# Experts of a mixture: every token through all four experts, or tokens sorted by expert into 19 tiles with weights copied for each tile

## The chip, the cores and the metric

One Trainium2 chip; the kernel runs on one of its cores. The metric is the device time of one execution in microseconds (us). The kernel before takes 2626.05 us (median of 3 runs, 2625.26 to 2626.93).

## What is computed

The reference sends 2048 tokens of 128 channels through eight residual layers: softmax attention, a spline feed-forward, retention, the spline again, linear attention, a conv-attention layer with a mixture of experts, an RWKV layer, and the conv-attention layer with the experts a second time (same weights). All is float32. The change concerns the mixture, which runs twice:

```
h = layernorm(x)                        # 2048 x 128
expert_idx = argmax(h @ router_w)       # one of E = 4 experts for each token
for e in range(E):
    gv = h @ expert_wv[e]               # 128 -> 2 * 512: gate and value
    gate_raw, value = split(gv, 2)
    y = gate_raw * sigmoid(gate_raw) * value @ expert_proj[e]   # 512 -> 128
    out = out + where(expert_idx == e, y, 0)
```

Only the output of the token's own expert counts.

## The kernel before

The program is a sequence of blocks; in each, the five engines have their own instruction streams, joined by semaphores, and all engines meet at a block's end. Tokens lie as NT = 16 tiles of 128 rows. `experts_stage` (L2018) is one such block and is called twice from `conv_moe_layer` (L2254), the first time followed by the RWKV layer, the second time by `store_stage`.

Its steps. **Norm**: VectorE and ScalarE normalise `moe_y` into `h`, TensorE transposes `h` (L377) into four banks, ScalarE writes them out as `h_t` (called ln_t in the profile, L346). **Router**: 16 small products `h_t` x `router` (L2049) give `logits_ps`; VectorE picks the expert of each token (L2107 to L2114: the maximum, then three chained operations for each expert) as a 0/1 mask `pick`. **Experts**: a loop over NQ = 4 blocks of 512 tokens, unrolled once and then a hardware loop; in it the 4 experts, and for each NF = 4 slices of 128 of the 512 hidden units. Each slice is one product for gate (L2067) and one for value (L2068), both with `expert_wv` in the array and 512 tokens streamed; ScalarE applies Silu (L2094), VectorE multiplies by value (L2147) into `hidden`. After the four slices the down product (L2057) puts 16 products of 128x128x128 into `expert_ps`; VectorE multiplies them by the token's `pick` and adds them into `X` (L2125, four instructions). So all 2048 tokens go through all 4 experts:

```
2067  nc.tensor.matmul(gp[g % 2][:], w["expert_wv"][:, e, f * P:(f + 1) * P], rhs, start=True, stop=True)
2068  nc.tensor.matmul(vp[g % 2][:], w["expert_wv"][:, e, DFF + f * P:DFF + (f + 1) * P], rhs, start=True, stop=True)
2057  ins = nc.tensor.matmul(op[e % 2][:, s * P:(s + 1) * P], hid[:, e % 2, f, s * P:(s + 1) * P],
                             w["expert_proj"][:, e % E, f, :], start=f == 0, stop=f == NF - 1)
2125  nc.vector.scalar_tensor_tensor(xi, op[e % 2][:, s * P:(s + 1) * P], pick[:, bass.ds(i, 1), e % E], xi, ALU.mult, ALU.add)
```

What sets the order is the text of each engine's stream: the down product of an expert stands after slice 1 of the next one, gate and value have two banks each, `hidden` two buffers. GpSimd adds `moe_y` into `X` once (L2084). SyncE has nothing to do in this block. The statistics for the next norm (L2136, L254) close the block. All weights are in SBUF from the first block on (loaded from GpSimd's queue, L832).

`spline_ffn_stage` (L1208) is another block, called twice; SyncE is idle in it as well.

## Time and profile before

| | |
|---|---|
| median of 3 runs | 2626.05 us |
| the profiled execution's own time | 2619.52 us |
| its span, first to last instruction | 2617.8 us |
| TensorE / VectorE / ScalarE / GpSimd busy | 83% / 69% / 53% / 14% |
| granted TensorE clock, mean | 0.918 |
| first experts block, from its first gate product to the next block | 1641.3 to 1816.1 us |
| second one, to the store of the result | 2438.3 to 2612.3 us |

A line of the page's fifth part, or of a view of lines, gives: source line, engine, operation, output<-inputs, shapes, count | busy time, mean ns | idle time of that engine before it and what ended it. In a timeline a line is: start, duration, engine, source line, operation, count [idle before <-releaser]. "PEld" is the weight load of a matmul, "issue" a wait for nothing that the profile shows, and a name with q (SPq, PEq) is an engine's instruction queue. A float32 product appears as two matmul instructions.

### The profile page before, as it was taken

The page shows a single profiled execution, that of the slowest core. Times are in us where ns is not written, and L with a number is a line of the kernel's source. Part 1 is how long each engine was busy: PE and PEld are TensorE (multiplying, and loading weights), DVE is VectorE, ACT ScalarE, POOL GpSimd, SP SyncE. Part 2 cuts the span into 40 slices and gives each one's busy share as a digit, 9 for nine tenths or more (in the row PEclk, how much of TensorE's full clock was granted, in tenths as well). Part 3 has the DMA queues.
Part 4 walks back from the last instruction along what each step waited for, and adds up shares of the span by engine and source line. Part 5 has one row for each costly group of instructions (what it writes and reads, how often), then busy time and mean ns, then how long its engine had stood idle before and what let it go on. Part 6 is the DMA issues. An engine that isn't in the chain of part 4 may idle for free. (4 is left out here: it accounts for less than half of the span.)

```text
span 2617.8 us, 39805 instructions
## 1 busy us (share of the span) xinstructions
PE 2182.6 (83%) x13356; PEld 951.5 (36%) x13356; DVE 1807.8 (69%) x4562; ACT 1384.6 (53%) x1981; POOL 354.5 (14%) x598
## 2 busy tenths in 40 slices
PE   3589999956799747758999998999448999999998
PEld 2123332224444335522233323665222233323665
DVE  7688788647477765678878874334968878884443
ACT  3246656772599743334566666223543566667222
POOL 4000010010355302100002001000000001001000
PEclk8799999987799868869999999999669999999899
DMA  7601010001111000160011000000151011000000
GB/s 196 140 1 38 2 38 1 1 1 36 40 46 49 23 0 1 28 185 13 2 37 38 1 1 1 1 0 0 28 161 37 1 38 34 6 1 2 1 1 16
DMA packets 46128, 81.67 MB, mean 31 GB/s; under 512 B 6132, under 2 KB 34164, under 8 KB 45284
## 3 DMA queue, kind: packets, MB, share of 16 engines
q1 hardware_dynamic: 40464, 70.46, 10.7%
q0 software_dynamic: 2528, 5.65, 0.8%
q10 hardware_dynamic: 2976, 3.55, 0.5%
q8 instruction: 85, 1.39, 0.2%
q14 instruction: 75, 0.61, 0.1%
HBM read 56.18 MB, written 23.07 MB: 30 GB/s over the span
## 5 line engine op out<-in xcount | busy, mean ns | idle before, releaser
L1026 ACT ACTIVATE probs<-score 128x1024 f32<-128x1024 f32 x960 | 825.7, 897 | 528.6 <-PE score L1090 525.4
L1148 DVE TENSOR_REDUCE max_part<-stat 128x1 f32<-128x512 f32 x1152 | 721.8, 683 | 120.2 <-PE stat L1040 118.8
L1103 PE MATMUL pv<-probs,v_ones 128*9 128x512 f32 (+3 forms) x3840 | 443.6, 534 | 0.7 <-ACT out_turned L1017 0.5
L1145 DVE CUSTOM_DVE_ANT_0 masked_scores<-stat,mask_row 128x128 f32<-128x128 f32 (+3 forms) x768 | 343.1, 487 | 101.5 <-PE stat L1040 100.1
L1040 PE MATMUL stat<-first_group_k,first_group_q 128*128 128x512 bf16 (+2 forms) x960 | 302.7, 370 | 78.7 <-DVE max_part L1148 34.2
L1000 POOL TENSOR_SCALAR_AFFINE_SELECT probs<-probs 128x256 f32<-128x256 f32 x384 | 154.8, 408 | 1254.7 <-ACT probs L1026 1251.3
L1040 PE MATMUL stat<-group_k,group_q 128*128 128x512 bf16 (+2 forms) x960 | 288.5, 349 | 15.0 <-DVE max_part L1148 8.9
L1090 PE MATMUL score<-first_group_q,first_group_k 128*128 128x512 bf16 x960 | 262.0, 356 | 15.7 <-DMA first_group_q<-row_max_turned 14.7
L1090 PE MATMUL score<-group_q,group_k 128*128 128x512 bf16 x960 | 253.9, 350 | 5.1 <-DMA group_q<-row_max_turned 2.8
L2094 ACT ACTIVATE gate<-gate_ps 128x512 f32<-128x512 f32 x128 | 76.4, 597 | 262.5 <-PE gate_ps L2067 262.5
L1040 PEld LDWEIGHTS stat<-first_group_k,first_group_q 128*128 128x128 bf16 x960 | 93.9, 99 | 262.0 <-DVE max_part L1148 123.3
L1740 ACT ACTIVATE abs_act_ps<-abs_act_ps 128x1024 f32<-128x1024 f32 (+3 forms) x176 | 167.5, 952 | 27.2 <-PE abs_act_ps L1693 27.0
L2147 DVE TENSOR_TENSOR hidden<-value_ps,gate 128x512 f32<-128x512 f32 x128 | 88.4, 691 | 109.0 <-PE value_ps L2068 108.5
L1090 PEld LDWEIGHTS score<-first_group_q,first_group_k 128*128 128x128 bf16 x960 | 72.8, 98 | 237.8 <-ACT probs L1026 107.9
L1040 PEld LDWEIGHTS stat<-group_k,group_q 128*128 128x128 bf16 x960 | 92.7, 97 | 164.7 <-DVE max_part L1148 67.6
L1090 PEld LDWEIGHTS score<-group_q,group_k 128*128 128x128 bf16 x960 | 69.3, 97 | 221.5 <-ACT probs L1026 169.4
L1774 DVE TENSOR_REDUCE abs_part<-abs_dve_ps 128x512 f32 (+5 forms) x224 | 108.5, 515 | 45.3 <-PE abs_dve_ps L1707 44.2
L2067 PE MATMUL gate_ps<-ln_t,expert_wv 128*128 (+1 forms) x256 | 134.7, 608 | 0.2
L2068 PE MATMUL value_ps<-ln_t,expert_wv 128*128 (+1 forms) x256 | 132.7, 600 | 0.0
L2057 PEld LDWEIGHTS expert_ps<-expert_proj,hidden 128*128 128x128 f32 x1024 | 119.2, 192 | 17.7 <-issue 17.7
L2057 PE MATMUL expert_ps<-expert_proj,hidden 128*128 128x128 f32 x1024 | 119.6, 275 | 1.8 <-DVE hidden L2147 1.8
L1693 PE MATMUL abs_act_ps<-head_k,head_q 128*128 128x512 bf16 x352 | 101.0, 374 | 7.0 <-ACT abs_act_ps L1740 4.0
(330 smaller groups left out, 2318.7 us busy)
## 6 DMA issues: line engine op xcount, KB each, us to landing
q_parts<-parts_t SPq DMA_DIRECT2D x40, 384.0 KB, 3.9
group_k<-k_parts SPq DMA_DIRECT2D x18, 384.0 KB
group_q<-q_parts SPq DMA_DIRECT2D x18, 384.0 KB
k_parts<-parts_t SPq DMA_DIRECT2D x16, 384.0 KB, 4.6
head_q<-q_parts SPq DMA_DIRECT2D x48, 96.0 KB
head_k<-k_parts SPq DMA_DIRECT2D x48, 96.0 KB
first_group_k<-k_parts SPq DMA_DIRECT2D x9, 384.0 KB
first_group_q<-q_parts SPq DMA_DIRECT2D x9, 384.0 KB
```

Source lines behind the costliest of these rows:

```text
L1000: nc.gpsimd.affine_select(tile, tile, [[0, 2], [1, P]], ALU.is_ge, 0.0, base=0, channel_multiplier=-1).then_inc(cut.sem, 1)
L1026: nc.scalar.activation(probs[:, n % PSLOTS, :, 0:width], sc[hp][:, :, 0:width], ACT.Exp, scale=scale).then_inc(expd.sem, 1)
L1040: last = nc.tensor.matmul(out[:, 0:width], uq[b][:, h, at:at + P], uk[b][:, h, c * BANK:c * BANK + width], start=True, stop=True)
L1090: last = nc.tensor.matmul(sc[hp][:, i, 0:BANK - f], uk[b][:, h, kt * P:(kt + 1) * P], uq[b][:, h, j * BANK + f:(j + 1) * BANK], start=True ...
L1103: last = nc.tensor.matmul(acc[32 * h:32 * h + D + 1, f:BANK], v9[:, kt, g * HG + h, :], probs[:, (2 * t + h // 2) % PSLOTS, h % 2, 0:BANK ...
L1145: nc.vector.tensor_tensor_reduce(masked[:, at % 2, 0:width], ring[n % RBANKS][:, 0:width], w["mask_row"][:, BANK - width:BANK], 1.0, NEG, ...
L1148: nc.vector.reduce_max(into, ring[n % RBANKS][:], AX.X).then_inc(stat_used.sem, 1)
L1740: nc.scalar.activation(ps, ps, ACT.Abs, accum_out=part[:, bass.ds(h, 1), i, 0:1]).then_inc(a_used.sem, 1)
L1774: nc.vector.tensor_reduce(part[:, bass.ds(h, 1), i, slot:slot + 1], d_ps[n % DRING][:, 0:width], AX.X, ALU.add, apply_absolute_value=True) ...
L2057: ins = nc.tensor.matmul(op[e % 2][:, s * P:(s + 1) * P], hid[:, e % 2, f, s * P:(s + 1) * P], w["expert_proj"][:, e % E, f, :], start=f = ...
L2067: nc.tensor.matmul(gp[g % 2][:], w["expert_wv"][:, e, f * P:(f + 1) * P], rhs, start=True, stop=True).then_inc(upped.sem, 1)
L2068: nc.tensor.matmul(vp[g % 2][:], w["expert_wv"][:, e, DFF + f * P:DFF + (f + 1) * P], rhs, start=True, stop=True).then_inc(upped.sem, 1)
```

## The change

Both calls of `experts_stage` are rewritten. After the router, VectorE and two small products (with `keep_kq` and with a matrix of ones) compute for each token a slot in an order sorted by expert, in which each expert begins at a multiple of 128, and for each of SLOTS = 19 tiles the expert that owns it (`owner`). GpSimd scatters the rows of `h`, each with its token's number as a 129th element, into a DRAM buffer of 2432 rows: 16 indirect DMAs of 128 rows. SyncE reads them back sorted (5 DMAs). TensorE transposes them, ScalarE applies the norm's affine. Then 19 tiles: SyncE reads the owner into a register and copies that expert's 512 KB of `expert_wv` from SBUF to one of four SBUF buffers; TensorE reads the owner too, makes 8 products of 128x128x128 for gate and value and 4 for the output; ScalarE and VectorE do one Silu, one product and one copy; GpSimd scatters the tile's 128 output rows to a second DRAM buffer at the token's number, by the numbers read back with the rows. At the end SyncE reads 2048 rows (4 DMAs) and VectorE adds them to `x`. Rows that no token fills carry numbers from 2048 up, so they land behind the part that is read; these numbers come from an input that SyncE copies, in the first spline block, into both DRAM buffers (2 x 1.26 MB, DRAM to DRAM). The add of `moe_y` moves from GpSimd to VectorE. The loop is fully unrolled and 19 tiles are always run, however the tokens fall. The diff, cut:

```diff
+SLOTS = NT + E - 1
...
+            @block.sync
+            def _(sp):
+                for dst, rows in copies:
+                    sp.dma_start(dst.rearrange("(p a) c -> p (a c)", p=P), rows.rearrange("(p a) c -> p (a c)", p=P)).then_inc(copied.sem, 16)
+                if copies:
+                    sp.wait_ge(copied.sem, copied.at(16 * len(copies)))
+
...
+        ones = k.sb("ones", [P, P], F32, ctx)
+        steps = k.sb("tile_numbers", [P, SLOTS], F32, ctx)
+        rows = k.sb("sorted_rows", [P, SLOTS, C + 1], F32, ctx)
+        rows_t = k.sb("sorted_t", [P, SLOTS * P], F32, ctx)
...
-        hid = k.sb("hidden", [P, 2, NF, BANK], F32, ctx)
+        hid = k.sb("hidden", [P, 2, BANK], F32, ctx)
+        outs = k.sb("expert_rows", [P, SLOTS, C], F32, ctx)
+        back = k.sb("token_rows", [P, NT, C], F32, ctx)
+        wv = k.sb("tile_wv", [P, WBUFS, 2 * DFF], F32, ctx)
         lp = k.ps("logits_ps", [P, BANK], ctx)
...
+            @block.sync
+            def _(sp):
+                sp.dma_start(steps[:], w["tile_numbers"].partition_broadcast(P)).then_inc(numbered.sem, 16)
+                with nc.allow_non_contiguous_dma(reason="a number for each row"):
+                    sp.dma_start(h[:, :, C], w["token_numbers"]).then_inc(numbered.sem, 16)
+
+                def load_wv(j):
+
+                    e = sp.value_load(owner[0:1, j:j + 1], min_val=0, max_val=E - 1)
+                    if j >= WBUFS:
+                        sp.wait_ge(upped.sem, upped.at(2 * (j - WBUFS) + 2))
+                    sp.dma_start(wv[:, j % WBUFS, :], w["expert_wv"][:, bass.ds(e, 1), :].rearrange("p o f -> p (o f)")).then_inc(wv_in[j % WBUFS].sem, 16)
+
+                sp.wait_ge(owner_ready.sem, owner_ready.at(1))
+                for j in range(WBUFS):
+                    load_wv(j)
+                sp.wait_ge(sorted_out.sem, sorted_out.at(16 * NT))
+                by_tile = sorted_dram.rearrange("(j p) c -> p j c", p=P)
+                for b in range(NB):
+                    js = slice(block_tiles(b)[0], block_tiles(b)[-1] + 1)
+                    sp.dma_start(rows[:, js, :], by_tile[:, js, :]).then_inc(rows_in[b].sem, 16)
+                for j in range(WBUFS, SLOTS):
+                    load_wv(j)
+                sp.wait_ge(returned.sem, returned.at(16 * SLOTS))
+                for q in range(NQ):
+                    ts = slice(QC * q, QC * q + QC)
+                    sp.dma_start(back[:, ts, :], out_dram[0:T].rearrange("(t p) c -> p t c", p=P)[:, ts, :]).then_inc(rows_in[q].sem, 16)
+
+            @block.gpsimd
+            def _(pool):
+                nc.gpsimd.memset(ones[:], 1.0).then_inc(ranked.sem, 1)
+                pool.wait_ge(numbered.sem, numbered.at(32))
+                pool.wait_ge(slot_ready.sem, slot_ready.at(1))
+                norm.wait_rows(pool)
+                for i in range(NT):
+                    nc.gpsimd.indirect_dma_start(sorted_dram, bass.IndirectOffsetOnAxis(ap=slot[:, i:i + 1], axis=0), h[:, i, :], None).then_inc(sorted_out.sem, 16)
+                for j in range(SLOTS):
+                    pool.wait_ge(rows_in[j // QC].sem, rows_in[j // QC].at(16))
+                    pool.wait_ge(out_ready.sem, out_ready.at(j + 1))
+                    nc.gpsimd.indirect_dma_start(out_dram, bass.IndirectOffsetOnAxis(ap=rows[:, j, C:C + 1].bitcast(I32), axis=0), outs[:, j, :], None).then_inc(returned.sem, 16)
...
+                pe.wait_ge(counted.sem, counted.at(1))
+                pe.wait_ge(ranked.sem, ranked.at(1))
+                nc.tensor.matmul(lp[:, NT * E:NT * E + E], w["keep_kq"][:], count[:], start=True, stop=True)
+                nc.tensor.matmul(lp[:, NT * E + E:NT * E + 2 * E], ones[:], count[:], start=True, stop=True).then_inc(ranked.sem, 1)
+
+                def turn(b):
+                    pe.wait_ge(rows_in[b].sem, rows_in[b].at(16))
+                    if b > 0:
+                        pe.wait_ge(kept.sem, kept.at(b))
+                    for s, j in enumerate(block_tiles(b)):
+                        ins = nc.tensor.transpose(tp[:, s * P:(s + 1) * P], rows[:, j, 0:C], w["ident"][:])
+                    ins.then_inc(turned.sem, 1)
+
+                def up(j):
+                    pe.wait_ge(wv_in[j % WBUFS].sem, wv_in[j % WBUFS].at(16 * (j // WBUFS + 1)))
+                    if j >= 2:
+                        pe.wait_ge(hid_ready.sem, hid_ready.at(j - 1))
+                    for bank, first in ((gp[j % 2], 0), (vp[j % 2], DFF)):
                         for f in range(NF):
-                            ins = nc.tensor.matmul(op[e % 2][:, s * P:(s + 1) * P], hid[:, e % 2, f, s * P:(s + 1) * P],
-                                                   w["expert_proj"][:, e % E, f, :], start=f == 0, stop=f == NF - 1)
+                            ins = nc.tensor.matmul(bank[:, f * P:(f + 1) * P], wv[:, j % WBUFS, first + f * P:first + (f + 1) * P], rows_t[:, j * P:(j + 1) * P], start=True, stop=True)
+                        ins.then_inc(upped.sem, 1)
+
+                def down(j, e):
+                    pe.wait_ge(hid_ready.sem, hid_ready.at(j + 1))
+                    if j >= 2:
+                        pe.wait_ge(out_ready.sem, out_ready.at(j - 1))
+                    for f in range(NF):
+                        wgt = w["expert_proj"][:, bass.ds(e, 1), f, :].rearrange("p o c -> p (o c)")
+                        ins = nc.tensor.matmul(op[j % 2][:, 0:C], hid[:, j % 2, f * P:(f + 1) * P], wgt, start=f == 0, stop=f == NF - 1)
                     ins.then_inc(downed.sem, 1)
 
...
+                turn(0)
+                pe.wait_ge(owner_ready.sem, owner_ready.at(1))
+                before = None
+                for j in range(SLOTS):
+                    e = pe.value_load(owner[0:1, j:j + 1], min_val=0, max_val=E - 1)
+                    if j % QC == 0:
+                        pe.wait_ge(kept.sem, kept.at(j // QC + 1))
+                    up(j)
+                    if j % QC == 1 and j // QC + 1 < NB:
+                        turn(j // QC + 1)
+                    if j > 0:
+                        down(j - 1, before)
+                    before = e
+                down(SLOTS - 1, before)
...
-            @block.gpsimd
-            def _(pool):
-                norm.wait_read(pool)
-                nc.gpsimd.tensor_tensor(x[:], x[:], y[:], ALU.add).then_inc(added.sem, 1)
...
+                def keep(b):
+                    js = block_tiles(b)
+                    act.wait_ge(turned.sem, turned.at(b + 1))
+                    nc.scalar.activation(rows_t[:, js[0] * P:(js[-1] + 1) * P], tp[:, 0:len(js) * P], ACT.Identity,
+                                         bias=norm.affine[1][:, 0:1], scale=norm.affine[0][:, 0:1]).then_inc(kept.sem, 1)
+
+                keep(0)
+                for j in range(SLOTS):
+                    act.wait_ge(upped.sem, upped.at(2 * j + 1))
+                    if j >= 4:
+                        act.wait_ge(hid_ready.sem, hid_ready.at(j - 3))
+                    nc.scalar.activation(gate[:, j % 4, :], gp[j % 2][:], ACT.Silu).then_inc(gated.sem, 1)
+                    if j % QC == 1 and j // QC + 1 < NB:
+                        keep(j // QC + 1)
...
+                nc.vector.tensor_reduce(count[:], pick[:], AX.X, ALU.add).then_inc(counted.sem, 1)
+                dve.wait_ge(numbered.sem, numbered.at(32))
+                dve.wait_ge(ranked.sem, ranked.at(2))
+                upto, total = lp[:, NT * E:NT * E + E], lp[:, NT * E + E:NT * E + 2 * E]
+                chain(nc.vector.tensor_copy(begin[:], total))
+                chain(nc.vector.scalar_tensor_tensor(over[:], bcast(steps[:, 0:NT], 1, E), float(P), bcast(begin[:], 2, NT), ALU.mult, ALU.is_lt))
+                chain(nc.vector.tensor_reduce(tiles[:], over[:], AX.X, ALU.add))
+                chain(nc.vector.tensor_tensor_scan(ends[:], ones[:, 0:E], tiles[:], 0.0, ALU.mult, ALU.add))
+                chain(nc.vector.tensor_tensor(begin[:], ends[:], tiles[:], ALU.subtract))
+                chain(nc.vector.scalar_tensor_tensor(begin[:], begin[:], float(P), upto, ALU.mult, ALU.add))
+                chain(nc.vector.tensor_tensor(begin[:], begin[:], count[:], ALU.subtract))
+                for e in range(E):
+                    ins = nc.vector.tensor_tensor_scan(place[:, e, :], ones[:, 0:NT], pick[:, e, :], begin[:, e:e + 1], ALU.mult, ALU.add)
+                chain(ins)
+                chain(nc.vector.tensor_tensor(place[:], place[:], pick[:], ALU.mult))
+                chain(nc.vector.tensor_reduce(at[:], place[:].rearrange("p e t -> p t e"), AX.X, ALU.add))
+                nc.vector.tensor_scalar(slot[:], at[:], -1.0, None, ALU.add).then_inc(slot_ready.sem, 1)
+                chain(nc.vector.tensor_tensor(passed[:], bcast(steps[0:1, :], 2, E - 1), bcast(ends[0:1, 0:E - 1], 1, SLOTS), ALU.is_ge))
+                chain(nc.vector.tensor_reduce(owner_f[:], passed[:], AX.X, ALU.add))
+                nc.vector.tensor_copy(owner[:], owner_f[:]).then_inc(owner_ready.sem, 1)
+                nc.vector.tensor_tensor(x[:], x[:], y[:], ALU.add).then_inc(added.sem, 1)
+
+                def take(j):
+                    dve.wait_ge(downed.sem, downed.at(j + 1))
+                    nc.vector.tensor_copy(outs[:, j, :], op[j % 2][:, 0:C]).then_inc(out_ready.sem, 1)
+
+                for j in range(SLOTS):
+                    dve.wait_ge(gated.sem, gated.at(j + 1))
+                    dve.wait_ge(upped.sem, upped.at(2 * j + 2))
+                    if j >= 2:
+                        dve.wait_ge(downed.sem, downed.at(j - 1))
+                    nc.vector.tensor_tensor(hid[:, j % 2, :], vp[j % 2][:], gate[:, j % 4, :], ALU.mult).then_inc(hid_ready.sem, 1)
+                    if j > 0:
+                        take(j - 1)
+                take(SLOTS - 1)
...
-                        nc.vector.scalar_tensor_tensor(xi, op[e % 2][:, s * P:(s + 1) * P], pick[:, bass.ds(i, 1), e % E], xi,
-                                                       ALU.mult, ALU.add).then_inc(out_used.sem, 1)
...
+                for q in range(NQ):
+                    ts = slice(QC * q, QC * q + QC)
+                    dve.wait_ge(rows_in[q].sem, rows_in[q].at(32))
+                    nc.vector.tensor_tensor(x[:, ts, :], x[:, ts, :], back[:, ts, :], ALU.add).then_inc(completed.sem, 1)
+                    stats.follow(dve, q, completed)
...
+        sorted_dram = [nc.dram_tensor(f"sorted_rows{n}", (SLOTS * P, C + 1), F32, kind="Internal").ap() for n in range(2)]
+        out_dram = nc.dram_tensor("expert_rows", (T + SLOTS * P, C), F32, kind="Internal").ap()
...
-        spline_layer(k, w, x)
+        spline_layer(k, w, x, [(s, d["c_unused_rows"]) for s in sorted_dram])
...
+        "c_tile_numbers": np.arange(SLOTS, dtype=np.float32),
+        "c_token_numbers": np.ascontiguousarray(np.arange(T, dtype=np.int32).reshape(NT, P).T).view(np.float32),
+        "c_unused_rows": np.concatenate([np.zeros((SLOTS * P, C), np.int32), T + np.arange(SLOTS * P, dtype=np.int32)[:, None]], 1).view(np.float32),
```

## Rows read from the trace of the kernel before

**Rows 1.** Page, first part: busy us of each engine (share of the span) xinstructions.
```profile
PE 2182.6 (83%) x13356; PEld 951.5 (36%) x13356; DVE 1807.8 (69%) x4562; ACT 1384.6 (53%) x1981; POOL 354.5 (14%) x598
```
**Rows 2.** Windows, both experts blocks: stretch, length, engines' busy us, granted clock, DMA share, GB/s.
```profile
1641.30:1816.10 174.80, 171.15 (x770) 106.72 (x769) 70.07 (x175) 39.70 (x66) 0.00 (x0) 0.98 0.00 0
2438.30:2612.30 174.00, 170.21 (x769) 106.23 (x768) 70.11 (x175) 39.71 (x66) 0.00 (x0) 0.99 0.00 0
```
**Rows 3.** Chain that ended last, in order of time, second block: start, us, what.
```profile
2438.34 1.91 PE gate_ps L2067 x2
2440.25 1.71 PE value_ps L2068 x2
...
2461.25 3.57 PE expert_ps L2057 x32
2464.82 0.86 PE gate_ps L2067 x2
...
2471.69 3.57 PE expert_ps L2057 x32
```
**Rows 4.** Waits, longest first, 1615 to 1780 us: who waited for whom, us, times, longest.
```profile
ACT gate L2094 <- PE gate_ps L2067: 108.5, 53, 4.7
DVE hidden L2147 <- PE value_ps L2068: 44.9, 47, 2.0
```
**Rows 5.** Timeline of VectorE in the picking of the experts, second block.
```profile
2438.89 0.19 DVE L2112 TENSOR_TENSOR pick<-logits,best 128x16 f32<-128x16 f32 x1
2439.11 0.19 DVE L2113 TENSOR_TENSOR pick<-pick,not_picked 128x16 f32<-128x16 f32 x1
```
**Rows 6.** Timeline, TensorE: a stretch at half clock, then transposes at full clock.
```profile
552.11 2.07 PE L465 MATMUL project<-wT,turned 128*128 128x128 f32 x8
553.98 1.01 PE L457 MATMUL turn<-ident,qkv 128*128 128x128 f32 x4
...
1622.31 0.60 PE L457 MATMUL turn<-ident,qkv 128*128 128x128 f32 x4
```
**Rows 7.** Windows: granted clock (third from the right) in stretches of one kind.
```profile
552.00:554.00 2.00, 2.00 (x11) 1.89 (x10) 0.00 (x0) 0.65 (x2) 0.00 (x0) 0.50 0.04 8
1655.00:1660.00 5.00, 5.00 (x35) 4.04 (x35) 1.68 (x5) 0.60 (x1) 0.00 (x0) 1.00 0.01 3
1140.00:1145.00 5.00, 0.00 (x0) 0.00 (x0) 0.59 (x1) 0.88 (x3) 0.00 (x0) 0.50 1.05 362
24.00:32.00 8.00, 3.45 (x14) 1.83 (x12) 3.90 (x8) 6.43 (x13) 8.00 (x15) 1.00 0.98 249
```
**Rows 8.** Timeline of GpSimd: DMAs that it issues.
```profile
13.69 0.54 POOL L832 DMA_DIRECT2D raw_weights<-in_L_attn_b_Wk  x1
32.10 1.18 POOL L832 DMA_DIRECT2D expert_proj<-in_L_ffn_expert_proj  x1
```
**Rows 9.** DMA issues: out<-in, queue, count, KB each, us from issue to landing.
```profile
q_parts<-parts_t SPq DMA_DIRECT2D x40, 384.0 KB, 3.9
out<-X SPq DMA_DIRECT2D x1, 1024.0 KB, 5.1
```
**Rows 10.** The instructions of tile X and of tile parts_t: landing times, last line of each.
```profile
DMA to landing us min/median/max: 5.1/5.8/6.5
DMA to landing us min/median/max: 2.6/4.0/6.8
```
**Rows 11.** Timeline: the last norm operations before the spline block and the block after it.
```profile
562.66 0.17 DVE L307 TENSOR_SCALAR ln_std<-row_mv 128x16 f32<-128x16 f32 x1 [0.60 <-DVEq L447]
605.77 0.18 DVE L307 TENSOR_SCALAR ln_std<-row_mv 128x16 f32<-128x16 f32 x1 [0.32 <-PEq L1222]
```
**Rows 12.** Timeline: what closes the second block.
```profile
2609.57 1.13 DVE L2125 SCALAR_TENSOR_TENSOR X<-expert_ps,pick,X 128x128 f32<-128x128 f32 x4 [3.18 <-PE expert_ps L2057]
...
2612.30 0.42 SPq L2179 DMA_DIRECT2D out<-X  x1
```
**Rows 13.** Lines of VectorE: an operation on two SBUF inputs, mean ns behind the comma.
```profile
L760 DVE TENSOR_TENSOR qkv<-qkv,cos 128x1024 f32<-128x1024 f32 x8 | 9.8, 1225 | 0.3
```

152 lines of the change are left out of this document (62 added, 90 removed).

## The prediction

> **What bounds the kernel now.** I read the page first: TensorE is busy for 83% of the span, more than any other engine [rows 1]. Then the windows over the two experts blocks: of 174.8 and 174.0 us TensorE works 171 and 170, at a granted clock of 0.98 and 0.99, while VectorE has 70 us of work, ScalarE 40, GpSimd and the DMA engines none [rows 2]. The list of waits says the same from the other side: ScalarE and VectorE wait for the gate and value products [rows 4]. So inside these blocks the time is TensorE's work, and the chain gives its prices [rows 3]: a gate or value product (128x128 weights, 512 tokens) 0.86 us, the down product of an expert (16 products of 128x128x128, 32 instructions) 3.57 us, so 0.1116 us an instruction. One expert on one block of 512 tokens is 8 x 0.86 + 3.57 = 10.44 us, as the two down products 10.44 us apart show, and a block of the program has 16 of them: 167.1 us. The first products are slow (1.91 and 1.71 us in place of 0.86: about 2 us lost), the rest is the end. Everything outside the two blocks is some 2270 us that the change hardly touches.
>
> **What it removes.** All 16 x 10.44 us, the start and the end: the 174.4 us of a block (mean of rows 2) are replaced whole. What comes instead has four stretches one after another.
>
> **1. Routing to slots.** The picks stay, minus one. A chained VectorE operation on 16 columns comes every 0.22 us [rows 5]: copy, maximum, 11 picks, count are 14 x 0.22 = 3.1. Two small products (4 instructions) with the engine at half clock: the transposes behind eight such instructions began 553.98 - 552.11 = 1.87 us after them, 0.23 each [rows 6], in a stretch at clock 0.50 [rows 7]; 4 x 0.23 and a hop there and back are 1.2. Then 14 more operations: 3.1. Sum 7.4 us. The token numbers (2048 pieces of four bytes) are asked for at the block's start, 13 us before the router is done; I cost them at nothing, covered by the norm. If that cover is too short, every us late is a us here. The owner of the tiles and the add of `moe_y` (2 x 1.225 = 2.5 us [rows 13]) come behind the slots on VectorE, beside GpSimd's work: nothing.
>
> **2. Scatter and read back.** GpSimd issues 16 indirect DMAs in a row. The trace has none. A plain DMA of 128 rows costs GpSimd 0.54 us, the one with the most pieces (`expert_proj`, 16 runs of 512 B for each partition) 1.18 us [rows 8]. An indirect one must also read 128 numbers and make 128 addresses; I take 1.18, the dearer row, 18.9 us in all, with 0.54 as the low end; upwards no row bounds it (see the third rival). The last must land: 3.9 us, as stores of `q_parts` to DRAM [rows 9], between 2.6 and 6.8 [rows 10]. SyncE's wait for it holds its five row loads; 3.9 us for the first. Then four transposes at 0.25, and ScalarE's pass: 1.9 with the hops. Sum 18.9 + 3.9 + 3.9 + 1.9 = 28.6 us. The first four weight copies (2 MB) start in this stretch; at the 249 GB/s of rows 7 they take 8.4 us, hidden.
>
> **3. Nineteen tiles.** Each has 12 products of 128x128x128, 24 instructions: 24 x 0.1116 = 2.68 us, 50.9 in all. Fifteen transposes at 0.15 [rows 6] are 2.2, the slow start 2. Nothing else on TensorE should be on the path: gate and value of tile j+1 (1.79 us) stand between those of j and the down product of j, and Silu and the multiply need about 1.3 us. VectorE has 0.69 + 0.3 us a tile, GpSimd 1.2. Reading the owner into a TensorE register is not in the trace. It is covered by the 0.89 us of the down product that is queued; between nothing and the 2.6 us of the shortest DMA in rows 10 I take 1.2, so 0.3 sticks out: 5.7 us, ends 0 and 32. The weight copies: 512 KB and the 64 KB of a scatter at 249 GB/s are 2.4 us a tile, less than the 3.1 of this sum, and four buffers give each copy three tiles of lead, so SyncE's waits for freed buffers hold up nobody. Sum 50.9 + 2.2 + 2 + 5.7 = 60.8 us.
>
> **4. The end.** The last copy 0.3, the issue 1.2, landing in DRAM 5.1 (the store of the result [rows 9]), four loads of 256 KB that together are the load of X: 6.5 [rows 10], an add of 0.69, statistics 0.87 + 0.38 [rows 12] and hops 0.3: 15.3 us. SyncE's last wait holds these loads, which wait for all 19 scatters.
>
> **The sum** is 7.4 + 28.6 + 60.8 + 15.3 = 112.1 us against 174.4: 62.3 less, twice 124.6. The two copies in the first spline block (2.5 MB, 10 us at 249 GB/s, counting each byte once, 20 twice) have 43 us between the two norms [rows 11], with a SyncE that is idle; nothing, unless they run on few DMA engines. From the profiled execution's 2619.5 us this leads to 2494.9; its time lies 6.5 us under the median, so against the median of 2626.05 I forecast **2501 us**. About 0.2% (5 us) is what a measurement of this kernel can tell from no change.
>
> The rows let VectorE's add of `moe_y` and GpSimd's scatters run side by side, since no row shows them together. The Trainium skill's page "SBUF — State Buffer", section "Who interferes with whom", says that a VectorE instruction with two SBUF inputs contends with a GpSimd instruction that reads SBUF. By it the scatters would stand still for those 2.5 us in each block, and the sum would be 2506.
>
> **The forecast's own range.** Low: scatters at 0.54 (-10.2), register read hidden (-5.7), landings of 2.6 (-3.8): 19.7 a block, 2462. High: a register read of 2 us (+15 a block) or scatters at 1.9 (+12): 2530.
>
> **Rivals.**
> *Weights set the pace.* All DMA rates here are between DRAM and SBUF. The copies go from SBUF to SBUF; if that passes the same side of the memory twice and runs at half of 249 GB/s, a tile needs 4.7 us instead of 3.2. 19 x 1.5 = 29 a block: 2559. For: 512 KB for 2.7 us of work is near the rate of rows 7. Against: another stretch there ran at 362 GB/s.
> *The clock.* TensorE stands still for 30 us in stretch 2, and in the tiles it may wait a little each time. Where it had no work, the granted clock was 0.50, the 1.2 GHz level [rows 7]; the first products of the block now ran at it and then rose [rows 3]. If it doesn't rise, a tile is 24 x 0.23 = 5.5 us in place of 2.68: 19 x 2.8 = 54 a block, 2609. Against: an engine that is its own bound is busy throughout. The Trainium skill tells of this in "TensorE: Matmul & The Clock Gate", section "HAM oscillation", of a kernel that waited for DMA in each round and started each one cold; by it this case comes with the first rival, as it stands.
> *Slower.* GpSimd's cost p of an indirect DMA stands in the path 16 times, and from about 3.2 us on it paces the tiles too: a block is then 7.4 + 9.7 + 2 + 14.1 + 36 p. It equals the 174.4 us of now at p = 3.9 us. At 5 us a block takes 213: 2704. For: software makes 128 addresses each time, and no row shows it. Against: the dearest DMA issue of rows 8 is 1.18 us.
> *No change*, because the change doesn't do what it says: should the DRAM-to-DRAM copies run on one engine of 16 (249 / 16 = 15.6 GB/s, 161 us), the spline block grows by 118 and nearly all is given back: 2619. That the tiles don't save work is excluded, since 19 are run whatever the tokens are.
>
> **How the numbers follow.** Forecast 0.62, weights 0.18, clock 0.10, slower 0.06, copies exposed 0.04. The time is the forecast's. The range goes from the low end just worked out, 2460, past the weights' case to 2595; it leaves out the clock, the slow scatter and the exposed copies, 0.2 together. Faster by over 0.2%: 0.62 + 0.18 + 0.10 and half of the copies' case, 0.92; same 0.02; slower 0.06.
>
> **What would show it.** The scatters' issues on GpSimd 1.2 us apart between the slots and SyncE's row loads; the first tile's product some 36 us after the router; products of one tile every 3 to 3.2 us; clock near 1.0 behind the first two tiles; a spline block as long as now. TensorE waiting for `tile_wv` means the first rival, a clock of 0.50 in the tiles the second, GpSimd's issues over 3 us apart the third. The prediction is wrong if a block takes over 150 us or under 92.

## The result and the profile after

| | before | after |
|---|---|---|
| median (4 runs each, side by side) | 2626.49 us (2625.26 to 2630.1) | **2485.8 us** (2480.75 to 2501.3) |
| ratio, 95% interval | | 0.9472 [0.9428, 0.9516] |
| profiled execution, own time / span | 2619.52 / 2617.8 us | 2488.74 / 2487.0 us |
| first experts block, from one norm's `ln_std` to the next | 187.3 us | 117.9 us |
| an experts block from the router's end [rows 2] | 174.8, 174.0 us | 105.1, 104.7 us |

The kernel is 5.3% faster; 2501 us was forecast, 2460 to 2595 as the range. Here is the page's first part of the kernel after, which answers to [rows 1]:

```profile
PE 1956.2 (79%) x12778; PEld 851.6 (34%) x12778; DVE 1734.1 (70%) x4426; ACT 1338.5 (54%) x1901; POOL 416.4 (17%) x668
```

TensorE lost 226 us of work, but the kernel only 131 (profile against profile): TensorE now waits inside the blocks. The windows, the same view as [rows 2, 7], are the two whole blocks, then the scatters, then the tiles:

```profile
1649.30:1754.40 105.10, 57.42 (x479) 56.55 (x479) 33.39 (x106) 17.90 (x27) 35.43 (x35) 0.76 0.38 139
2376.80:2481.50 104.70, 57.20 (x479) 56.34 (x479) 33.42 (x106) 17.89 (x27) 35.39 (x35) 0.76 0.39 140
1660.00:1680.00 20.00, 0.00 (x0) 0.00 (x0) 0.00 (x0) 0.00 (x0) 14.58 (x16) 0.50 0.39 142
1695.00:1735.00 40.00, 40.00 (x361) 40.00 (x360) 14.30 (x30) 10.59 (x17) 13.42 (x14) 1.00 0.50 196
```

So 57 us of TensorE work in 105 us. While GpSimd scatters, TensorE does nothing and its clock stands at 0.50; in the tiles it is busy the whole 40 us at clock 1.00, with the DMA engines half busy. What releases what at the start of the first block is in the timeline of the kernel after:

```profile
1656.30 0.17 DVE L2233 TENSOR_SCALAR slot<-place 128x16 int32<-128x16 f32 x1
...
1656.94 2.27 DVE L2237 TENSOR_TENSOR X<-X,moe_y 128x2048 f32<-128x2048 f32 x1
1657.36 2.83 POOL L2121 DMA_INDIRECT sorted_rows<-ln,slot  x1 [20.62 <-DVE slot L2233]
...
1660.49 0.98 POOL L2121 DMA_INDIRECT sorted_rows<-ln,slot  x1 [0.30 <-issue]
1661.78 0.96 POOL L2121 DMA_INDIRECT sorted_rows<-ln,slot  x1 [0.30 <-issue]
...
1678.19 0.96 POOL L2121 DMA_INDIRECT sorted_rows<-ln,slot  x1 [0.30 <-issue]
1680.47 2.60 SPq L2106 DMA_DIRECT2D sorted_rows<-sorted_rows  x5
1683.33 1.11 PE L2148 MATMUL sorted_ps<-ident,sorted_rows 128*128 128x128 f32 x4 [29.91 <-DMA sorted_rows<-sorted_rows]
1685.31 2.08 PE L2157 MATMUL gate_ps<-sorted_t,tile_wv 128*128 128x128 f32 x8 [0.87 <-ACT sorted_t L2191]
```

Read it as a relay: the slots are ready at 1656.47; sixteen scatters follow, the first of 2.83 us, the others 1.26 us apart (0.96 of work and 0.30 of "issue"); 2.3 us after the last one was begun its rows are in DRAM and SyncE reads them back; 2.9 us later TensorE turns them, and the first gate product starts 36.0 us after the router's end. The chain that ended last shows the second block's end (start, us, what):

```profile
2465.82 0.91 PE expert_ps L2166 x8
...
2467.80 0.48 POOL expert_rows L2125
...
2469.06 2.25 DMA expert_rows<-expert_rows,sorted_rows
2471.33 0.37 SPq L2112
...
2472.29 4.22 DMA token_rows<-expert_rows
...
2476.53 0.69 DVE X L2256
```

Put beside the prediction's four stretches, second block (the middle boundary is the first gate product, at 2412.80; the last product ended at 2467.9, the store was issued at 2481.49):

| stretch | predicted | measured |
|---|---|---|
| 1. Routing to slots | 7.4 | 7.2 |
| 2. Scatter and read back | 28.6 | 28.8 |
| 3. Nineteen tiles | 60.8 | 55.1 |
| 4. The end | 15.3 | 13.6 |
| sum | 112.1 | 104.7 |

Two blocks save 139 us. The profiled execution saved 131: the other 8 are in blocks that the change doesn't touch (the first softmax block 549.5 us in place of 546.6, the softmax of the conv layer 543.1 in place of 537.4). These blocks differ as much between the kernels measured here, none of which changes them: the first softmax block takes 546.5 to 551.8 us, the softmax of the conv layer 535.1 to 549.1. The last experiment bears on that.

### The profile page after: what moved, and what is told of

It is laid out like the page before. It is cut to its first block and busy times, and to the rows that moved or that the text cites. A ratio compares the mean times of both kernels' runs of the same rounds, so it can differ in the third digit from the quotient of the medians.

```text
span 2487.0 us, 38310 instructions
## 1 busy us (share of the span) xinstructions
PE 1956.2 (79%) x12778; PEld 851.6 (34%) x12778; DVE 1734.1 (70%) x4426; ACT 1338.5 (54%) x1901; POOL 416.4 (17%) x668
## 5 line engine op out<-in xcount | busy, mean ns | idle before, releaser
L2248 DVE TENSOR_TENSOR hidden<-value_ps,gate 128x512 f32<-128x512 f32 x38 | 26.3, 691 | 115.6 <-PE value_ps L2157 115.6
L1109 PEld LDWEIGHTS pv<-probs,v_ones 128*9 128x9 f32 x3840 | 57.3, 88 | 112.6 <-issue 91.7
L1662 POOL TENSOR_SCALAR own_positive<-own_scores 128x2048 f32<-128x2048 f32 x16 | 85.7, 5358 | 0.0
L1722 PE MATMUL abs_dve_ps<-head_k,head_q 128*128 128x512 bf16 (+2 forms) x224 | 66.7, 314 | 0.6
L1151 DVE DVE_READ_ACCUMULATOR2_ANT max_part<- 128x1 f32 x768 | 63.6, 83 | 0.1
L1177 DVE RECIPROCAL inv_denominator<-stat 128x16 f32<-128x16 f32 x48 | 12.4, 257 | 69.4 <-PE stat L1056 68.7
```

Source lines behind the costliest of these rows:

```text
L1109: last = nc.tensor.matmul(acc[32 * h:32 * h + D + 1, f:BANK], v9[:, kt, g * HG + h, :], probs[:, (2 * t + h // 2) % PSLOTS, h % 2, 0:BANK ...
L1151: nc.vector.tensor_tensor_reduce(masked[:, at % 2, 0:width], ring[n % RBANKS][:, 0:width], w["mask_row"][:, BANK - width:BANK], 1.0, NEG, ...
L1662: nc.gpsimd.tensor_scalar(sa[:, par, :], sm[:, par, :], 0.0, None, ALU.max).then_inc(abs_ready.sem, 1)
L1722: ins = nc.tensor.matmul(out[:, 0:width], qm[:, par, i * P:(i + 1) * P], km[:, par, at:at + width], start=True, stop=True)
```

## The experiments

Each time is to be compared with that of the kernel before on the same chip: its median is 2621.2 us for `e_add_later`, `e_scatter_twice`, `e_weights_twice` and `e_warm`, 2622.29 for `e_no_copies`, `e_reads_8`, `e_best` and `e_before_copies`, 2619.88 for `e_reads_2`, `e_no_register`, `e_warm_110` and `e_both_120`. "The block" is the first experts block between two `ln_std`: 117.9 us in the kernel after. It shows what a total hides, since the softmax blocks vary by several us. "The second block" runs from its `ln_std` to the store of the result: 117.4 us. Each kernel has one trace, so a block time is one execution; where a total has no number of runs beside it, it is of one run too.

### Stretch 2: what paces the scatters

`e_scatter_twice`: another scatter before each, into the other DRAM buffer.

```diff
                 for i in range(NT):
+                    nc.gpsimd.indirect_dma_start(out_dram, bass.IndirectOffsetOnAxis(ap=slot[:, i:i + 1], axis=0), h[:, i, 0:C], None).then_inc(sorted_out.sem, 16)
                     nc.gpsimd.indirect_dma_start(sorted_dram, ...)
```

> Before each of the 16 scatters of the sort a second one sends the same 128 rows (128 of 129 elements) by the same slots to the other DRAM buffer, where the results overwrite them later. Theory: GpSimd's issue sets the pace, 0.96 us and 0.30 between two, so 16 more cost 20.2 us a block and the time is about 2526. Rival, transfers set it: the DMA engines, which also carry the first four weight copies, fall behind with 32 scatters in a row; the issues get dearer than 1.26 us or the last landing longer than 2.3 us, and the time is over 2535.

Measured: 2531.33 us, the block 138.6 us, 20.7 more (the second 21.0 more). The timeline of this run has the scatters 1.26 us apart to the last, and SyncE's loads 2.3 us behind its start:

```profile
1696.01 0.96 POOL L2122 DMA_INDIRECT sorted_rows<-ln,slot  x1 [0.30 <-issue]
...
1698.30 2.67 SPq L2106 DMA_DIRECT2D sorted_rows<-sorted_rows  x5
```

Sixteen scatters cost 16 x 1.26 = 20.2 us, so the stretch is paced by GpSimd's issue, and one landing is paid whatever their number.

`e_add_later`: VectorE's add of `moe_y` (two SBUF inputs) moved out of the first scatter's way, behind the multiply of tile 4.

```diff
-                nc.vector.tensor_tensor(x[:], x[:], y[:], ALU.add).then_inc(added.sem, 1)
...
+                    if j == 4:
+                        nc.vector.tensor_tensor(x[:], x[:], y[:], ALU.add).then_inc(added.sem, 1)
```

> VectorE's add of moe_y into X (128x2048, 2.27 us) moves from behind the tiles' owners to behind the multiply of tile 4. In the changed kernel the first scatter of each block takes 2.83 and 2.82 us, the 15 others 0.96, and the add runs beside the first. Theory, contention: the first scatter waits for the add. Then it falls to 0.96 us, each block gets 1.9 us shorter, the time goes from 2486 to about 2482, and the scatter of tile 3, which now stands beside the add, takes about 2.8 us, hidden. Rival, first use: the first indirect DMA of a block is dear by itself; it stays at 2.8 us and the time stays at 2486.

Measured: 2485.89 us (4 runs), ratio 0.9471 [0.945, 0.9492], the block 116.6 us (-1.3), the second 115.1 (-2.3). In the timeline of this run the first scatter is now short, and the result scatter that runs beside the moved add (1695.64, 2.28 us) is long:

```profile
1652.94 1.10 POOL L2121 DMA_INDIRECT sorted_rows<-ln,slot  x1 [20.62 <-DVE slot L2233]
...
1696.48 2.27 POOL L2125 DMA_INDIRECT expert_rows<-expert_rows,sorted_rows  x1 [1.72 <-DVE expert_rows L2240]
1699.60 0.96 POOL L2125 DMA_INDIRECT expert_rows<-expert_rows,sorted_rows  x1 [0.84 <-DVE expert_rows L2240]
```

The slow scatter goes with the add, not with being first: it took 2.83 us beside it, 1.10 away from it, and another took 2.27 beside it. In the tiles this hides, as GpSimd had 1.72 us of idle time before each scatter. From the start of the first scatter to that of the last it is now 19.1 us in the first block and 19.0 in the second, against 20.8 in both: the add had cost 1.7 to 1.8 us. The blocks as wholes moved by 1.3 and 2.3, because the slow start of the tiles differs from block to block (see the clock, below). The total doesn't resolve either.

### Stretch 3: the weight copies

`e_weights_twice`: every copy is made twice, the second time into four more buffers that nobody reads; TensorE waits for both.

```diff
-                    sp.dma_start(wv[:, j % WBUFS, :], w["expert_wv"][...]).then_inc(wv_in[j % WBUFS].sem, 16)
+                    for buf in (wv, wv2):
+                        sp.dma_start(buf[:, j % WBUFS, :], w["expert_wv"][...]).then_inc(wv_in[j % WBUFS].sem, 16)
```

> Each tile's 512 KB of weights are copied twice, the second time to buffers that no product reads; the tile waits for both. In the changed kernel the tiles come every 2.68 us and the DMA engines are busy for 0.50 of the time at 196 GB/s. Theory, room to spare: 1.1 MB for a tile need a share of about 0.95, so the pace stays at 2.68 us, or a little above; the time is 2486 to 2500. Rival, the rate seen elsewhere (249 GB/s) is a ceiling: a tile then takes 4.5 us, 19 x 1.8 = 34 us more in each block, 2554.

Measured: 2492.95 us, the block 118.2 us (+0.3), the second 117.5 (+0.1). The windows of this run in the tiles, which answer to the fourth of the kernel after:

```profile
1700.00:1740.00 40.00, 40.00 (x361) 40.00 (x360) 14.43 (x29) 10.85 (x18) 14.19 (x15) 1.00 0.93 357
2424.00:2464.00 40.00, 40.00 (x361) 40.00 (x361) 13.95 (x29) 11.07 (x18) 13.76 (x15) 1.00 0.99 384
```

TensorE is still busy for 40 of 40 us with the DMA engines at 0.93 and 0.99 of their time. 384 GB/s passed, nearly all of it from SBUF to SBUF. But the doubled load fits only because the tiles end first: late in the first block SyncE issues its pairs of copies 2.86 us apart (five steps from 1717.94 to 1732.26), against 2.68 us for a tile, so the lead of the four buffers was being used up. The single load keeps the DMA engines busy for half of the time.

`e_no_copies`: no copies; in every tile the gate and value products read expert 0's weights in place, so this kernel leaves out the choice of the expert there.

```diff
-                        wv[:, j % WBUFS, first + f * P:first + (f + 1) * P]
+                        w["expert_wv"][:, 0, first + f * P:first + (f + 1) * P]
```

> No weight copies: the gate and value products of every tile read expert 0's weights where they lie, so the output is wrong for the other experts; the down product still goes by the owner. Theory: the copies are hidden, in the wait for the sorted rows and in the tiles, so the tiles stay at 2.68 us and a block keeps its 118 us (norm of this block to norm of the next). Rival: beside the scatters and the row loads the copies cost something, or SyncE's register reads hold the row loads back; then the first scatters' landing (2.3 us) and the row load (2.9 us) get shorter, by up to 1 us a block.

Measured: 2478.43 us, the block 117.4 us, the second 118.3. TensorE waited 30.05 us for the sorted rows, against 29.91 with the copies: they are hidden from both sides.

### Stretch 3: reading the owner into a TensorE register

`e_reads_8` and `e_reads_2` read it eight times and twice, `e_no_register` not at all on TensorE's queue (its down products take expert 0's weights in every tile).

```diff
-                    e = pe.value_load(owner[0:1, j:j + 1], min_val=0, max_val=E - 1)
+                    for _n in range(8):        # e_reads_2: range(2); e_no_register: e = 0
+                        e = pe.value_load(owner[0:1, j:j + 1], min_val=0, max_val=E - 1)
```

> TensorE's queue reads each tile's owner into a register eight times instead of once (0.3 to 0.9 us each, median 0.6). Theory, the read is hidden behind queued products: the multiply that the down product waits for ends 2.7 us before the next tile's gate products are due, so one read (0.6) costs nothing and eight (4.9 us) stick out by about 2.2 us a tile, 40 us a block, 2566 in all. Rival, the reads don't queue behind each other (they overlap, or are faster in a row): under 1 us a tile, below 2520. Rival, the prediction's cover (0.89 us): 4 us a tile, 2638.

Measured: 2625.41 us, the block 192.0 us: 74.1 more, 3.9 a tile. The instructions of that line on TensorE's queue in this run (count: min/median/max ns, first and last start), first of the whole run, then of 1693 to 1700 us, and two tiles of its timeline:

```profile
L2174 PEldq TENSOR_LOAD <-tile_expert x304: 293/301/904, 1674.1 to 2599.7; - x152
L2174 PEldq FUSED_REGOPS  x304: 146/146/165, 1674.7 to 2600.1; - x152
...
L2174 PEldq TENSOR_LOAD <-tile_expert x8: 295/296/895, 1693.7 to 1698.8; - x8
L2174 PEldq SEQ_ASSERT  x8: 18/18/18, 1694.2 to 1699.3; - x8
```

```profile
1692.90 1.13 PE L2157 MATMUL gate_ps<-sorted_t,tile_wv 128*128 128x128 f32 x8 [3.05 <-issue]
...
1694.76 1.06 PE L2166 MATMUL expert_ps<-expert_proj,hidden 128*128 x8
1699.50 2.04 PE L2157 MATMUL gate_ps<-sorted_t,tile_wv 128*128 128x128 f32 x8 [3.68 <-issue]
1701.34 1.91 PE L2157 MATMUL value_ps<-sorted_t,tile_wv 128*128 128x128 f32 x8
```

The load of 0.30 us and the register work of 0.15 are not all of a read: undisturbed, one begins 0.64 us after the last, and one of these eight held the queue for 1.2 us. From the first load (1693.7) to the last assert (1699.3) the eight take 5.7 us. When they began, TensorE still had products in its queue until 1695.8. So the queue was about 2 us ahead of the engine, and what it does in that time is free. The rest of the 5.7 us is the hole of 3.68. This tile, from gate product to gate product (1692.90 to 1699.50), took 6.60 us with every group at the full clock level, 3.9 more than 2.68: the cost is the queue's. Behind the hole the clock is at its lower level (groups of 2.04 and 1.91 us in place of 1.13 and 1.06), the queue is further ahead in time, and the next hole is 1.78 us; that tile took 7.23 us.

> TensorE's queue reads the expert of each tile twice instead of once (a read takes 0.30 to 0.9 us in the rows). If the cover is only one group of 8 products (0.89 us, the prediction's step), two reads of 0.6 us stick out by about 0.3 us a tile, 19 tiles: the block gains 5 to 6 us, about 123.5 us. If the cover is a whole tile of 2.68 us, nothing: 117.9 us within 1 us. Eight reads cost 3.9 us a tile, which lies nearer to the first.

Measured: 2490.05 us, the block 118.4 us (+0.5), the second 118.4 (+1.0). One hole, 0.23 us before the third tile's gate products, then none to speak of (TensorE 39.77 us busy in a 40 us window at clock 1.00).

> TensorE's queue no longer reads a tile's expert from the owner row: the weights of W_o are those of expert 0 in every tile (this leaves out the choice of the expert in the down projection; the weight copies still choose). My prediction put 0.3 us a tile, 5.7 us a block, on that read sticking out of its cover. Theory 'the queue runs ahead': the read lies wholly behind products that are already in the engine, so tiles stay 2.68 us and the block stays within 1 us of 117.9 us from norm to norm. Theory of the prediction: the block falls by 5.7 us, to 112.2 us. In the changed kernel the tiles already follow one another without a hole, so I expect the first.

Measured: 2491.22 us (2 runs), ratio 0.9503 [0.9469, 0.9536], the block 117.4 us (-0.5), the second 118.1 (+0.7). Together, first block and second: no read 117.4 and 118.1, one 117.9 and 117.4, two 118.4 and 118.4, eight 192.0 and 192.3. So no cost of one read can be told, and the cover holds two. Two reads take 1.2 to 1.9 us here, at least 0.64 apart, so a cover of 0.89 us, as the expectation of `e_reads_2` says, would have let them stick out. A cover of about 2 us holds them, and leaves 3.7 of the 5.7 us of eight. In the kernel after it is seen directly: a read begins at 1701.7, and the gate product behind it at 1703.68, without a hole.

```profile
1701.45 1.06 PE L2157 MATMUL value_ps<-sorted_t,tile_wv 128*128 128x128 f32 x8
1702.35 0.60 PE L2148 MATMUL sorted_ps<-ident,sorted_rows 128*128 128x128 f32 x4
1702.78 1.06 PE L2166 MATMUL expert_ps<-expert_proj,hidden 128*128 x8
1703.68 1.06 PE L2157 MATMUL gate_ps<-sorted_t,tile_wv 128*128 128x128 f32 x8
```

### The clock at the start of the tiles

`e_warm` puts 120 float32 products of 128x128x128 between the routing and the first turn, into a bank that is free; `e_warm_110` puts 110.

```diff
+                for n in range(120):
+                    nc.tensor.matmul(op[0][:, 0:C], w["expert_proj"][:, 0, n % NF, :], w["keep_kq"][:], start=True, stop=True)
                 turn(0)
```

> 120 products of 128x128x128 (240 matmul instructions, their result is never read) fill TensorE's 30 us of waiting before the sorted rows come; nothing else changes. In the changed kernel the clock is 0.50 there and the first gate and value groups take 2.07, 1.71 and 1.15 us where the later ones take 0.89. Theory, clock: with the engine busy the clock is 1.0 when the rows come, all groups take 0.89, the four transposes 0.6 in place of 1.1: some 2.7 us less in each block, about 2481 in all. Rival, start: the first groups are slow because the first use of buffers or instructions is; they stay as they are, 2486. A third outcome, the products last longer than the wait: the blocks get longer by what sticks out.

Measured: 2479.67 us (4 runs), ratio 0.9455 [0.9424, 0.9486], the block 115.3 us (-2.6), the second 114.9 (-2.5). The turn took 0.66 us in place of 1.11 and the first gate group 1.16 in place of 2.08. This is the timeline of that run:

```profile
1677.52 0.66 PE L2148 MATMUL sorted_ps<-ident,sorted_rows 128*128 128x128 f32 x4 [1.42 <-DMA sorted_rows<-sorted_rows]
1679.04 1.16 PE L2157 MATMUL gate_ps<-sorted_t,tile_wv 128*128 128x128 f32 x8 [0.87 <-ACT sorted_t L2193]
1680.04 1.06 PE L2157 MATMUL value_ps<-sorted_t,tile_wv 128*128 128x128 f32 x8
```

The tiles, from the first gate product to the end of the last product, took 53.1 us in both blocks of this run, and in both of `e_both_120` below. In the blocks that begin at the lower level, whose tiles are not held up by seven extra reads, they took 54.5 to 56.2 us. So the slow start costs about 1.4 to 3 us and differs from block to block; block differences of less than about 1 us tell nothing.

> 110 dummy products and the add of x left in its place. If the number of products (the place in the program) makes the holes, they are here: block 125 to 128 us. If the moved add makes them, this block is like that with 120 dummies, 115.3 us within 1 us. Both this and the run before without holes would mean that the cause is neither alone.

Measured: 2491.37 us (2 runs), ratio 0.9503 [0.947, 0.9537], the block 117.8 us: nothing gained. Ten products fewer end sooner, TensorE idles 2.53 us instead of 1.42 before the turn, and the products run at the lower level again, as this run's timeline shows:

```profile
1683.42 1.12 PE L2148 MATMUL sorted_ps<-ident,sorted_rows 128*128 128x128 f32 x4 [2.53 <-DMA sorted_rows<-sorted_rows]
1685.40 2.07 PE L2157 MATMUL gate_ps<-sorted_t,tile_wv 128*128 128x128 f32 x8 [0.87 <-ACT sorted_t L2193]
```

The expectation of 115.3 was wrong: it counted the dummies' work and not the idle time behind them.

### Both together, and a surprise

`e_best` is the edit of `e_add_later` with 110 dummy products, `e_both_120` the same with 120.

> Both edits that shortened a block together: VectorE's add behind tile 4's multiply, and 110 products (10 fewer, since the wait is 1.7 us shorter) that keep TensorE busy until the rows come. Theory, they add up: the block from norm to norm falls from 117.9 us by 1.3 + 2.6 to about 114, and the time from 2486 to about 2478. Rival, they overlap (the clock's gain is smaller once the wait is shorter, or the products now stick out): 2480 or more.

Measured: 2500.88 us (5 runs, 2497.21 to 2506.17), ratio 0.954 [0.9519, 0.9561]: slower than the kernel after, the block 127.6 us. In both blocks the dummies run for 11 to 12 us and then stutter, until 3 us after the end of the last scatter. The timeline of this run:

```profile
1665.98 0.49 PE L2170 MATMUL expert_ps<-keep_kq,expert_proj 128*128 128x128 f32 x3 [0.72 <-issue]
...
1673.06 1.10 PE L2170 MATMUL expert_ps<-keep_kq,expert_proj 128*128 128x128 f32 x4 [1.73 <-issue]
1675.89 0.59 PE L2170 MATMUL expert_ps<-keep_kq,expert_proj 128*128 128x128 f32 x2 [1.73 <-issue]
...
1680.15 15.83 PE L2170 MATMUL expert_ps<-keep_kq,expert_proj 128*128 128x128 f32 x116 [0.32 <-issue]
1695.81 0.60 PE L2148 MATMUL sorted_ps<-ident,sorted_rows 128*128 128x128 f32 x4
```

They end at 1695.8, some 15 us later than they would without the holes, and the turn stands behind them in TensorE's stream.

> The add of x moved behind the multiply of tile 4 and 120 dummy products on TensorE between the routing and the first turn: the same as the run with 110 dummies but for ten more of them. That one had holes of 0.7 to 1.7 us in the dummy products from about 10 us after their start until the scatters ended, 14 us in all, in both experts blocks, and was slower than the changed kernel; 120 dummies without the moved add had none. If the holes come with the place of the instructions in the program (fetching them), ten more products may well take them away: the block then costs 117.9 - 1.3 - 2.6 = 114.0 us from norm to norm and the kernel about 2478 us. If they come from the moved add (the scatters' start without contention), they stay: block 125 to 128 us, kernel about 2500 us.

Measured: **2479.9 us** (5 runs, 2471.26 to 2486.11), ratio 0.9461 [0.9435, 0.9487], the block 113.5 us: 4.4 less than the kernel after (the second 113.4, 4.0 less), about the sum of 1.7 for the scatters and 2.6 for the clock. No holes. Its timeline has the turn right behind the last dummy, at full clock:

```profile
1647.55 28.49 PE L2170 MATMUL expert_ps<-keep_kq,expert_proj 128*128 128x128 f32 x240
1675.90 0.66 PE L2148 MATMUL sorted_ps<-ident,sorted_rows 128*128 128x128 f32 x4
1677.42 1.16 PE L2157 MATMUL gate_ps<-sorted_t,tile_wv 128*128 128x128 f32 x8 [0.87 <-ACT sorted_t L2193]
```

So neither the moved add (`e_both_120` has it) nor the count of 110 (`e_warm_110` has it) makes the holes alone; they belong to the one program with both, in each of its five executions by their times. The profile calls them "issue", a wait for nothing that it shows. That TensorE's instructions came late, by where they lie in the program, would fit, but no run here shows it. It stays open.

### The copies in the spline block

`e_before_copies` is the kernel before with the two DRAM-to-DRAM copies in its first spline block.

```diff
-        spline_layer(k, w, x)
+        spline_layer(k, w, x, [(s, d["c_unused_rows"]) for s in sorted_dram])
```

> The kernel before with the two DRAM-to-DRAM copies of 1.26 MB in the first spline block, and with the input and the two DRAM buffers they need; the experts as before. In five profiles the first softmax block takes 549.5 to 551.8 us with the change and 546.6 without, though no line of it is changed. Theory: the copies end long before the block (landing 8 us of 43), so they cost nothing and the ratio to before is 1.000 within 0.002. Rival 1: the copies lengthen the spline block, from 43.1 us by 1 or more. Rival 2: what costs 3 us in the first softmax block is the larger set of DRAM buffers and inputs; then that block takes 549 or more here too, and the ratio is about 1.001.

Measured: 2622.23 us (12 runs), ratio 1.0001 [0.9987, 1.0016]; the spline block between its two norms 43.3 us, against 43.1. They cost nothing that can be told. (In the kernel after this block took 44.1 us, but the block behind it 321.0 in place of 323.1.) Here, with no change to the experts, the first softmax block took 549.8 us, and 546.5 in `e_no_copies` and 546.7 in `e_both_120`, which have the same copies and buffers: neither the copies nor the buffers make that drift. Whether it belongs to the program or to the one execution that was traced, no run shows; the totals of the kernel after alone spread from 2480.75 to 2501.3 us.

## Why the prediction was right, point by point

**The sum held, in its parts as well.** Two stretches came within 0.2 us, and the place of the first gate product, 36 us behind the router, was right. The saving was forecast as 62.3 us a block and measured as 69.5.

**1. Routing to slots: right**, 7.2 for 7.4. Its parts held too: 3.1 us for the picks, 1.1 for the two products with their hops, 3.0 for the rest, and VectorE waited for those products and not for the token numbers. What it left out is a hop of 0.8 us from the slots to GpSimd's first scatter; it is counted in stretch 2.

**2. Scatter and read back: right in sum by luck, since errors cancel.** Hop 0.8, fifteen periods 20.8, the last scatter and its landing 2.3, the row load 2.9, turn and keep 2.0: 28.8. I had 17.7 for fifteen, 5.1 for the last with its landing, 3.9 and 1.9. The price of 1.18 us from [rows 8] lay near the truth for the period of 1.26, although the instruction alone takes 0.96: the 0.30 between two belongs to the price. The landing came from [rows 9], a DMA of 384 KB; a scatter of 66 KB landed in 2.3 us from its start.

In the first scatter are 1.7 us beside VectorE's add (2.83 against 1.10 us), gone when the add is elsewhere. The prediction's sum allowed none and named 2.5. The Trainium skill's page "SBUF — State Buffer", section "Who interferes with whom", has the rule that a VectorE instruction with two SBUF inputs contends with a GpSimd instruction that reads SBUF; this case's traces agree with it, in two places.

**3. Nineteen tiles: the mechanism right, one term that isn't there.** 50.9 + 2.2 + 2 = 55.1 is what was measured in the second block, 55.3 in the first. The price of 0.1116 us an instruction, read off a down product of the kernel before [rows 3], holds for gate and value products cut to the same size: a group of eight comes every 0.89 us. That the sum fits to 0.1 us is in part luck: the fifteen transposes took 1.7 us, 0.11 each, the slow start 2.3, and like blocks spread from 54.5 to 56.2. The step that failed is "so 0.3 sticks out: 5.7 us": a tile came every 2.68 us and not every 3 to 3.2, and no cost of a read can be told from 0. What was wrong in it is "covered by the 0.89 us of the down product that is queued": the queue was about 2 us ahead of the engine, more than a down product, as `e_reads_8` and the kernel after show. The price of 1.2 us was the upper end of what a read takes (0.6 to 1.2 us), and even that lies under the cover. In the kernel after the reads stand on TensorE's queue as

```profile
L2173 PEldq TENSOR_LOAD <-tile_expert x38: 295/612/922, 1683.3 to 2461.9; - x38
```

with 0.15 us of register work and an assert behind each; the whole read takes 0.9 us in the median.

**4. The end: 1.7 us too long, again by opposite errors.** The last scatter, from its start to its landing, took 2.3 us where I had 1.2 + 5.1. The loads landed 2.8 to 4.4 us after their issues, and VectorE's first add began 2.9 us after the first of them, where I had 6.5 us for all four. But from there on VectorE has 7.0 us of its own work (four adds of 0.69 and the statistics of all four parts, 2474.26 to 2481.2), where I counted one add and one part; the loads hide behind it.

**The rivals.** *Weights set the pace* falls: twice the copies cost 0.3 us, at up to 384 GB/s; "half of 249 GB/s" for SBUF to SBUF was far off. *The clock* falls as a case, since the tiles ran at 1.00. In the wait of 30 us it stood at 0.50, the first groups took 2.08, 1.91 and 1.57 us, and keeping TensorE busy gave back 2.6 us. But the wait did not lower it: it was at 0.50 already in the 7.3 us of router products before, 7.24 of them busy, and the block of the kernel before began at 0.50 too and lost 2 us [rows 3]. The Trainium skill's page "TensorE: Matmul & The Clock Gate", section "HAM oscillation", speaks of a kernel whose waits start each round cold; the trace of the kernel after has no waits between the tiles, and only the first round is cold (0.50, then 1.00). *Slower*: the scatters repeat every 1.26 us, far under the 3.9 at which it begins. *No change*: the spline block took 44.1 us and not 161, and `e_before_copies` has the copies at no cost.

**The list of waits**, 1640 to 1760 us, as [rows 4], shows where the time goes: ScalarE waits for the gate products 34.6 us in place of 108.5; VectorE waits for the value products 57.9 us in place of 44.9, but 30.0 of them are the one wait until the first tile; and TensorE has the new wait for the rows.

```profile
DVE hidden L2248 <- PE value_ps L2157: 57.9, 19, 30.0
POOL expert_rows L2125 <- DVE expert_rows L2241: 45.1, 18, 14.6
ACT gate L2199 <- PE gate_ps L2157: 34.6, 19, 2.5
PE sorted_ps L2148 <- DMA sorted_rows<-sorted_rows: 29.9, 1, 29.9
```

## What to carry to other kernels

Where one engine's work is the block, count its instructions by the price of one of the same kind: a group of eight products came every 0.89 us, as the rows before the change said. For a queue of equal operations take the period and not the duration of one, and a landing once, from a DMA of like size. What an engine's own queue must do between two groups (a register read here) is free as long as work lies ahead of it, and very dear beyond: at two reads it cost 0.5 to 1 us a block, at eight 74. Read the cover off the trace, from the start of the queue's instruction to the end of the products before it, and the price from one read's start to the next, not from the duration of its load.

## What the runs showed that I had not expected

- An indirect DMA of 128 rows of 516 B occupies GpSimd for 0.96 us, plus 0.30 to the next, and its rows are in DRAM 2.3 us after its start.
- TensorE's queue ran about 2 us ahead of the engine (full clock), so a register read of 0.6 to 1.2 us in it costs nothing; 5.7 us of them cost 3.9 us a tile.
- SBUF-to-SBUF copies, with the scatters beside them, passed 384 GB/s beside products at full pace, at 0.99 of the DMA engines' time.
- Dummy products have to reach up to the real ones: with 1.42 us of idle time behind them the clock was kept, with 2.53 it was not. The length of one hole doesn't tell it alone, since in `e_reads_8` a group behind a hole of 3.05 us still took 1.13 us and one behind 3.68 took 2.04. 120 of them gain 2.5 to 2.6 us a block, with the moved add 4.0 to 4.4, and the kernel's total shows it only just: 2479.9 against 2485.8 us, with ratios of 0.9461 [0.9435, 0.9487] and 0.9472 [0.9428, 0.9516] that overlap. The shorter block is shown, a faster kernel is not.
- Holes of up to 1.7 us (2.2 in the second block) in a plain run of products (`e_best`), some 15 us in a block, that came and went with ten products more or a moved add. Their cause is not known.
